# Softmax denominators from ScalarE's accumulator, and queries turned before they are split

## The reference

```python
qs, ks, vs = (relu(t.reshape(bs, ts, 16, 32)) for t in (layernorm(x), ctx, ctx))
att = softmax(einsum('bthf,byhf->bhty', qs, ks) / sqrt(32))
out = einsum('bhty,byhf->bhtf', att, vs).reshape(bs, ts, -1)
x = x + tanh(g_xattn) * relu(out @ ffn_w.T + ffn_b)
# then, on layernorm(x): xr, xk = token-shift mixes
x = x + tanh(g_ffn) * sigmoid(xr @ W_r.T) * (square(relu(xk @ W_k.T)) @ W_v.T)
```

## Time and profile before

| what | value |
|---|---|
| three timed runs, median (lowest to highest) | 2979.16 us (2978.43 to 2980.26) |
| the profiled execution: time, span | 2980.25 us, 2978.4 us |
| TensorE, VectorE, ScalarE, GpSimd busy | 96%, 78%, 53%, 35% |
| mean granted TensorE clock | 0.993 |
| HBM traffic over the span | 137 GB/s |

### The profile page before, as it was taken

The page is one execution under the profiler, slowest core; times in us unless marked ns, Lnnn a source line. Parts: engine busy times, 40 slices in busy tenths (PEclk is TensorE's granted clock), DMA queues, the critical chain, the costliest instruction groups (busy, mean ns, idle before and its releaser), DMA issues.

```text
span 2978.4 us, 71298 instructions
## 1 busy us (share of the span) xinstructions
PE 2860.3 (96%) x23168; PEld 2190.6 (74%) x23168; DVE 2330.1 (78%) x4175; ACT 1564.3 (53%) x2828; POOL 1045.4 (35%) x902
## 2 busy tenths in 40 slices
PE   3899999999999999999999999999999999999998
PEld 2677777777777777777777777777777777777776
DVE  5777877878878878878877877877878778788774
ACT  4445555555455455555555555555555555554552
POOL 0233333333343343333333333333333333333434
PEclk9899999999999999999999999999999999999999
DMA  5544445445445445445445445455455454454431
GB/s 168 150 122 140 144 124 155 140 127 155 135 131 156 137 131 154 133 137 150 131 142 149 128 143 153 120 149 152 120 152 146 124 152 142 124 156 137 130 109 41
DMA packets 405258, 408.56 MB, mean 137 GB/s; under 512 B 164577, under 2 KB 329441, under 8 KB 405218
## 3 DMA queue, kind: packets, MB, share of 16 engines
q1 hardware_dynamic: 352994, 340.92, 39.6%
q10 hardware_dynamic: 52224, 67.12, 7.3%
HBM read 272.64 MB, written 134.22 MB: 137 GB/s over the span
## 4 chain that ended last, share of the span: by engine, by line
PE 59%; DVE 16%; DMA 10%; SPq 7%; issue 5%; ACT 1%; ACTq 1%; DVEq 0%; POOL 0%; POOLq 0%
PE bank L951 29%; DMA out_dram<-x 8%; PE bank L918 7%; PE bank L932 6%; PE bank L906 5%; PE bank L944 4%; DVE m_nat L699 4%; DVE o_val L718 4%; SPq L272 3%; DVE st L652 3%; DVE k_raw L682 2%; PE bank L893 2%; PE bank L875 2%; SPq L258 2%; SPq L270 2%
## 5 line engine op out<-in xcount | busy, mean ns | idle before, releaser
L496 ACT ACTIVATE probs<-bank 128x512 f32<-128x512 f32 x1024 | 596.4, 594 | 455.7 <-PE bank L918 228.1
L699 DVE TENSOR_REDUCE m_nat<-bank 128x2 fp32r<-128x512 f32 x1024 | 695.4, 685 | 107.4 <-PE bank L906 106.7
L477 ACT ACTIVATE q_st<-bank 96x512 fp32r<-96x512 f32 x512 | 304.1, 594 | 718.9 <-PE bank L875 718.8
L918 PE MATMUL bank<-q_st,k_st 97*128 97x256 f32 x2048 | 449.9, 301 | 64.2 <-ACT probs L496 47.4
L718 DVE RECIPROCAL o_val<-bank 128x256 f32<-128x256 f32 x256 | 449.1, 1754 | 56.1 <-PE bank L944 51.7
L918 PEld LDWEIGHTS bank<-q_st,k_st 97*128 97x128 f32 x2048 | 341.8, 191 | 153.8 <-issue 58.5
L906 PE MATMUL bank<-k_st,q_st 96*128 96x256 f32 x2048 | 431.6, 293 | 7.4 <-DMA k_st<-k_dram 4.8
L397 POOL TENSOR_TENSOR xm<-xm 128x512 f32<-128x512 f32 x128 | 133.3, 1041 | 787.2 <-ACT xm L540 787.2
L906 PEld LDWEIGHTS bank<-k_st,q_st 96*128 96x128 f32 x2048 | 358.2, 192 | 59.8 <-issue 6.2
L708 DVE CAST m_t<-bank 4x256 fp32r<-4x256 f32 x256 | 105.1, 411 | 285.5 <-PE bank L884 285.4
L364 POOL TENSOR_TENSOR o_lo<-o_mv,o_hi 128x512 fp32r<-128x512 f32 x128 | 164.8, 1287 | 430.0 <-ACT o_hi L503 430.0
(11 more groups left out here) (90 smaller groups left out, 6026.6 us busy)
## 6 DMA issues: line engine op xcount, KB each, us to landing
k_st<-k_dram SPq DMA_DIRECT2D x256, 256.0 KB, 3.6
k_raw<-ctx_t_dram SPq DMA_DIRECT2D x256, 128.0 KB, 3.0
x_ln<-x_dram SPq DMA_DIRECT2D x256, 128.0 KB
k_dram<-k_high SPq DMA_DIRECT2D x64, 512.0 KB, 3.0
k_dram<-k_raw SPq DMA_DIRECT2D x64, 512.0 KB, 4.5
k_st<-k_dram SPq DMA_DIRECT2D x256, 128.0 KB, 3.5
o_dram<-o_val SPq DMA_DIRECT2D x256, 128.0 KB, 1.7
o_mv<-o_dram SPq DMA_DIRECT2D x512, 64.0 KB, 2.2
```

What stands on the lines that cost most here:

```text
L477: nc.scalar.activation(q_st[0:QK, c, :, P * u:P * u + P], tp_bank[0:QK, :].rearrange("p (g t) -> p g t", g=GR), ACT.Copy).then_inc(q_stack ...
L496: nc.scalar.activation(probs[:, n // GR % 2, n % GR, :, :].rearrange("p v t -> p (v t)"), st_bank[n % 2][:, :], ACT.Exp, scale=SCALE).then ...
L699: nc.vector.tensor_reduce(m_nat[:, c % 2, :, n % GR:n % GR + 1], s_bank[n % 2][:, :].rearrange("p (u y) -> p u y", u=NU), AX_X, ALU.max, n ...
L918: mm = nc.tensor.matmul(st_bank[n % 2][:, T * v:T * v + T], k_st[0:ST, c, g, P * v:P * v + P], q_st[0:ST, c, g, :], start=True, stop=True)
```

## The change

**Denominators.** `denominators` is gone, `values` alone fills `pv_bank`. Instead ScalarE's new `sum_exp(b, n)` takes the exponent of the natural scores in place in `s_bank`, with the negated maximum as bias, once for each half of the tokens, and its accumulator output goes to a column of `den`. So a bank of scores is free for the next head only after `s_summed`, no longer after `s_maxed`. `recip` inverts the eight columns of a group, `turn_rden` turns them, `copy_rden` copies them out of the bank, SyncE writes them to `rden_dram` and reads them back spread over the rows (`rd_val`), and `norm_o` multiplies by that.

**Queries.** `norm_1` writes a reordered tile `q_low_t`, with the softmax scale in it (the variance is multiplied by 32). `turn_q` turns it unsplit, twice a round, four full tiles in fp32; `q_high` and `q_low` split it from the bank, and `write_q` and `stack_q` take both parts through `q_dram`, as the keys go.

**Maxima.** One turn for both halves of a group instead of two.

```diff
+            def sum_exp(b, n):
+                if on(b):
+                    act.wait_ge(s_maxed, HEADS * b + n + 1)
+                    c, g = n // GR, n % GR
+                    for u in range(NU):
+                        scores = s_bank[n % 2][:, T * u:T * u + T]
+                        last = nc.scalar.activation(scores, scores, ACT.Exp, bias=m_nat[:, c % 2, g, u:u + 1].bitcast(F32),
+                                                    accum_out=den[:, c, NU * g + u:NU * g + u + 1])
+                    last.then_inc(s_summed, 1)
...
             def q_high(b, u):
                 if on(b):
+                    act.wait_ge(q_turned, NU * b + u + 1)
+                    nc.scalar.activation(x_ln[:, u, :].bitcast(F32R), tp_bank[:, :], ACT.Relu).then_inc(q_hi_ready, 1)
...
+            def recip(b, c):
+                if on(b):
+                    dve.wait_ge(s_summed, HEADS * b + GR * c + GR)
+                    nc.vector.reciprocal(rden[:, c, :], den[:, c, :]).then_inc(rden_ready, 1)
...
-                    nc.vector.reciprocal(o_val[:, :], pv_bank[:, T:2 * T]).then_inc(rden_ready, 1)
-                    dve.wait_ge(rden_ready, CH * b + c + 1)
-                    nc.vector.tensor_tensor(o_val[:, :], pv_bank[:, 0:T], o_val[:, :],
+                    dve.wait_ge(rd_moved[c], 16 * (b + 1))
+                    nc.vector.tensor_tensor(o_val[:, :], pv_bank[:, 0:T], rd_val[:, c, :],
...
                 if on(b):
+                    pe.wait_ge(x_normed, NU * b + u + 1)
                     freed(*users)
+                    for c in range(KC):
+                        mm = nc.tensor.transpose(tp_bank[:, P * c:P * c + P],
+                                                 q_low_t[:, u, c, :],
+                                                 ident_r[:, :].bitcast(F32))
                     mm.then_inc(q_turned, 1)
...
-                    after(pe, s_maxed, HEADS * b + n - 1)
+                    after(pe, s_summed, HEADS * b + n - 1)
...
-                turns = [("q", i, 2, 1), ("m", i, 1, 0), ("q", i, 3, 0), ("q", i, 3, 1),
+                turns = [("m", i, 1), ("q", i + 1, 0), ("q", i + 1, 1), ("rden", i, 1), ("m", i, 2),
+                         ("rden", i, 2), ("x", i - 1, 0), ("m", i, 3), ("x", i - 1, 1), ("rden", i, 3),
+                         ("m", i + 1, 0), ("rden", i + 1, 0)]
...
                     if kind == "q":
-                        return q_stacked, b, 2 * CH, 2 * c + u + 1
+                        return q_lo_ready, b, NU, n + 1
```

More of the change, by code:

```diff
@@ L139, in flamingo_block @@
         q_turned = sem("q_turned")
-        q_stacked = sem("q_stacked")
+        q_written = sem("q_written")
+        q_stacked = [sem(f"q_stacked{c}") for c in range(CH)]
         v_ready = sem("v_ready")
@@ L152, in flamingo_block @@
         pv_ready = sem("pv_ready")
+        s_summed = sem("s_summed")
         rden_ready = sem("rden_ready")
+        rden_turned = sem("rden_turned")
+        rden_copied = sem("rden_copied")
+        rden_written = sem("rden_written")
+        rd_moved = [sem(f"rd_moved{c}") for c in range(CH)]
         o_ready = sem("o_ready")
@@ L931, in values @@
                             h = GR * c + g
-                            nc.tensor.matmul(pv_bank[HD * g:HD * g + HD, 0:T], v_pos[:, v, HD * h:HD * h + HD],
-                                             probs[:, c % 2, g, v, :], start=(v == 0), stop=(v == NU - 1))
-            def denominators(b, c):
-                if on(b):
-                    after(pe, o_ready, CH * b + c)
-                    sums = [[probs[:, c % 2, g, v, :] for g in range(GR)] for v in range(NU)]
-                    for n, per_head in enumerate(sums):
-                        for g, moving in enumerate(per_head):
-                            mm = nc.tensor.matmul(pv_bank[HD * g:HD * g + HD, T:2 * T], ones_r[:, 0:HD].bitcast(F32),
-                                                  moving, start=(n == 0), stop=(n == len(sums) - 1))
+                            mm = nc.tensor.matmul(pv_bank[HD * g:HD * g + HD, 0:T], v_pos[:, v, HD * h:HD * h + HD],
+                                                  probs[:, c % 2, g, v, :], start=(v == 0), stop=(v == NU - 1))
                     mm.then_inc(pv_ready, 1)
@@ L1059, in iteration @@
                 values(i - 1, 3)
-                turn(1)
-                denominators(i - 1, 3)
+                turn(0)
                 dense(0, 2)
@@ L1064, in iteration @@
                 dense(0, 3)
-                turn(2)
+                turn(1)
                 shifted_scores(i, 2)
@@ L1070, in iteration @@
                 dense(1, 1)
+                turn(2)
                 shifted_scores(i, 3)
-                turn(3)
                 dense(1, 2)
@@ L1076, in iteration @@
                 dense(1, 3)
+                turn(3)
                 shifted_scores(i, 4)
@@ L1088, in iteration @@
                 turn(4)
-                denominators(i, 0)
                 shifted_scores(i, 6)
-                turn(5)
                 dense(3, 0)
@@ L1105, in iteration @@
                 scores(i, 15)
-                turn(7)
                 dense(4, 1)
@@ L1127, in iteration @@
                 dense(5, 3)
-                turn(11)
+                turn(9)
                 shifted_scores(i, 12)
@@ L1137, in iteration @@
                 values(i, 2)
-                turn(12)
+                turn(10)
                 scores(i + 1, 4)
@@ L1144, in iteration @@
                 scores(i + 1, 5)
-                denominators(i, 2)
-                turn(13)
                 dense(7, 1)
@@ L1152, in iteration @@
                 dense(7, 3)
+                turn(11)
             pipeline(pe, iteration)
```

197 lines of the change are left out of this document (125 added, 72 removed).

## The result

The changed kernel takes 3493.72 us (median of four timed runs, 3471.76 to 3495.93), the kernel before 2978.80 in the same comparison: ratio 1.171, 95% interval 1.166 to 1.176. The forecast was 2865, and the range ended at 3015. The change makes the kernel slower by 17%.

The account below looks back on a forecast made before the run. TensorE's own work was taken as the bound, 44.27 of 44.95 us a round. Work of 38.8 plus waits of 2.2, 1.65 and 0.5 gave 43.15 us, hence 2865 us; range 2803 to 2958, with outer end 3015.

Parts of the forecast that it names:

- TensorE's work, 38.8 us a round: TensorE's own work after denominators and old query turns leave and new turns enter: 38.8 us, from 44.27.
- The summing exponent, 0.50 us: ScalarE's 32 new 128x256 exponents with accumulator output, taken at 0.50 us each, 16 us a round.
- Rival 2: Slower kernel because ScalarE's summing exponent is long; decides from 0.76 us each, up to 3086 us; chance 0.15.
- The two waits on the turning bank, 2.2 and 1.65 us: TensorE waits for VectorE's low part at the second query turn, 2.2 us, and the reciprocals' turn, 1.65 us.
- The third wait, 0.5 us: Scores two heads on wait for a sum where tanh, copies and the keys' relu load ScalarE: 0.5 us a round.
- the sum 38.8 + 2.2 + 1.65 + 0.5: TensorE's work plus three waits: 43.15 us a round, 1.8 less than 44.95.
- rival 4: Busy DMA engines and SyncE's 55 in-order transfers land the query stack late; 2993 us at 8.5 us landing; chance 0.07.
- Rival 3, the clock: Idle gaps lower TensorE's clock; 1.8 us of work a round at 1.2 GHz eats the gain; chance 0.09.
- The wait at 1043.93 left the clock at 1.00: Argument against the clock loss: TensorE's existing 0.64 us wait for ScalarE's exponent had not lowered the clock.
- The forecast's own first wait, 2.2 us: TensorE at the second query turn, waiting for VectorE's low part to free the turning bank: 2.2 us a round.
- DMA share 0.7 to 0.75: DMA engines' busy share with 3.0 MB more a round: 32 of 43 us, 75%; sign of being right: near 0.7.
- That alone is no bound: Claim that DMA engines busy 32 of 43 us a round, 75%, do not by themselves limit the kernel.

Follow-up runs that it names:

- e10: Changed kernel without the reciprocals' DRAM trip and the division, maxima moved by ScalarE's queue, four query calls early: 3063.91 us, ratio 1.028.
- e8: Kernel before with ScalarE's sums replacing the denominators, old queries, no DRAM trip, division left out: 3137.71 us, ratio 1.053.
- e4: Kernel before with the queries' new way alone, denominators still by TensorE: 3236.19 us, ratio 1.086.
- e12: e8 with three of the four small copies of turned sums moved forward on VectorE: 3087.83 us, ratio 1.036.
- e1: Changed kernel without the reciprocals' trip through DRAM, multiplying by ones, so the division is left out: 3181.45 us, ratio 1.068.
- e2: Changed kernel with SyncE's order alone changed: reads behind the next move of maxima, loads behind the last: 3303.54 us, ratio 1.109.
- e3: Changed kernel with the four moves of maxima issued from ScalarE's queue instead of SyncE's: 3494.73 us, ratio 1.173.
- p1: Kernel before with TensorE paused once a round until one small ScalarE operation behind head 4's exponent is done: 3251.87 us, ratio 1.092.
- e13: e8 with sums ahead of each slot's exponent and three of the four small copies moved forward: 3083.07 us, ratio 1.034.

## Why the prediction was wrong, step by step

**TensorE's work, 38.8 us a round: about right.** The changed kernel shows 42.6 at a clock of 0.94. Taking 0.06 x 53.1 = 3.2 us off for the clock leaves 39.4. e10 leaves 40.0. Of the 5.5 us of work that the forecast took off (44.27 to 38.8; its 6.2 held 0.7 of idle time too), 4.3 to 4.9 are seen to go. e8 shows less, 2.5 of the 3.9 us expected of it (42.3 less 0.5 for the clock, against 44.3). Part of what is missing may be only how busy time is counted: in e4's timeline a matmul of 0.28 us is followed by the next after 0.12, but before a gap it counts whole. With over seven gaps a round in e8 instead of one, that is about 1 us, an estimate that no run checks.

**The summing exponent, 0.50 us: right.** Two groups of the page, the exponent and its read-out, and two neighbours in ScalarE's timeline:

```profile
L551 ACT ACTIVATE bank<-bank,m_nat 128x256 f32<-128x256 f32 x2048 | 921.4, 453 | 169.1 <-DVE m_nat L767 168.8
...
L551 ACT ACTIVATION_READ_ACCUMULATOR bank<-bank,m_nat 128x1 f32 x2048 | 434.2, 212 | 0.0
```

```profile
1507.22 0.45 ACT L551 ACTIVATE bank<-bank,m_nat 128x256 f32<-128x256 f32 x1
1507.58 0.20 ACT L551 ACTIVATION_READ_ACCUMULATOR bank<-bank,m_nat 128x1 f32 x1
1507.67 0.45 ACT L551 ACTIVATE bank<-bank,m_nat 128x256 f32<-128x256 f32 x1
```

From start to start it is 0.45 us with the read-out, which largely lies beside the exponent. Rival 2 (0.76 us and more) did not happen. ScalarE comes to 2180.8 / 64 = 34.1 us a round, 35.4 in the forecast.

**The two waits on the turning bank, 2.2 and 1.65 us: right in place and cause, 2.1 and 1.0 in size.** The tenth of a microsecond at the first is partly luck. In the round shown TensorE is ready for the turn 8.1 us after the round's first shifted score instead of 7.6, and starts it 10.4 us after instead of 9.8, because the two normalisations take 1.3 us instead of 0.9 and TensorE had stood 0.26 at the first query turn. At the second the chain from turn to turn took 3.9 us for the 4.0 worked out, but the work that TensorE has in between ran partly at the lower clock and filled more of it (a wait of 0.19 us there, 1.0 on average).

**The third wait, 0.5 us: small in the changed kernel** (8.6 us over the span), because other waits give ScalarE time. In e12 it is 3.1 us, but e12 keeps the old queries' copies, with 37.9 us of ScalarE's work a round against 34.0 here. e10, with the new queries, runs as fast as e12 and shows 8.7 us over the span. So what it would be in the whole change at the forecast's pace is open.

**The step that failed: the sum 38.8 + 2.2 + 1.65 + 0.5 had no term for the wait on the row of maxima.** It had only the two waits on the bank and one on the sums. SyncE's 55 transfers instead of 35 were counted in rival 4, and there only for the stack of queries, with a chance of 0.07. The move of the maxima stands in the same queue, is needed within the round, and cost 6.6 us a round. Two things were left out of its walk: that SyncE stops at each read-back until its write has landed (746.0 us over 254 reads, 2.9 each), and that the row, once issued, takes 2.3 to 5.9 us to land among the loads. The landing of the keys and the issue of the maxima were both at hand; the chain from copy to shifted scores was never made from them. Relieving the queue (e1) gave 312 us and reordering it (e2) 190, while taking only the maxima out of it (e3) gave nothing: it is what the whole queue has to do in a round, and in which order. Rival 4's own object, the stack of queries, held TensorE for only 18.2 us over the span. The Trainium skill, DMA: Bandwidth & Descriptors, section "Anatomy of one DMA — SWDGE (gpsimd) path", says for another path that the fixed cost of a transfer is mostly the confirmation that its last byte has landed, slowest in HBM. These writes carry 8 rows of 512 bytes and are still waited for 2.9 us on average; the trace does not separate the confirmation from the time behind other transfers, and the write issued at 1528.80, behind four loads, held SyncE until 1535.09.

**Rival 3, the clock: dismissed on a row that could not decide it.** "The wait at 1043.93 left the clock at 1.00" was true of 0.64 us. The forecast's own first wait, 2.2 us, is nearly as long as p1's pause, and that cost 1.8 us beyond its length. The wait of 2.31 us in the changed kernel is followed by slices at 0.63 and 0.80, 3 x 0.37 + 3 x 0.20 = 1.7 us. So with no surprise in SyncE's queue the sum comes to 43.15 + 1.7, about 44.9 us, an estimate: no gain worth the name. The rival's arithmetic was right (1.8 us of work at the lower level eats the gain), its chance of 0.09 was the error. In the changed kernel the clock took about 3.2 us a round. That is an estimate from its mean; the same working gives 2.5 for p1 (0.05 x 49.5), where the busy time grew by 2.0.

**The sum again**, from what was measured: 38.8 + 0.6 + 3.2 (clock) + 10.6 (waits) = 53.2 us against 53.1; 8.1 us more than before over 64 rounds are about 520 us, for 515 measured. The 0.6 is what the busy time and the clock's estimate leave over, so the sum closes by its making; what it shows is the sizes. The two terms that the forecast did not have, 6.6 us for the maxima and 3.2 for the clock, are 9.8 of the 10.0 us between 43.15 and 53.1; the smaller differences cancel.

**DMA share 0.7 to 0.75: 0.62,** because the same bytes are spread over a longer round: 0.62 x 53.1 = 32.9 us of all engines, where 32 had been worked out. **"That alone is no bound": right**, since e10 runs faster at 0.67.

**What stays open.** Whether any order of the whole scheme reaches the kernel before was not shown. The runs above tried few orders. e10 and e13 leave out the division and still end 3% above it, each with 4.6 to 5.6 us of idle TensorE a round in several pieces. That dropping the denominators takes work off TensorE is shown by the busy times (2.0 to 2.5 us a round in e8); that it can be had as time is not.

## What to carry to other kernels

Before pricing work that leaves the bounding engine, walk every chain that feeds it back to where it starts, in-order DMA queues included, and for each queue list what now stands ahead of the one small transfer that the bound waits for. In a round with no slack, a read that must wait for its own write belongs on a queue where nothing urgent stands behind it. And price a wait on TensorE at more than its length: here a gap of 2.5 us cost 4.3.

## What the runs showed of the hardware

- Gaps of 2.31, 3.11, 4.18 and 2.55 us were followed by slices of 3 us with a granted clock of 0.63, 0.50, 0.56 and 0.60, that is partly at 1.2 GHz, although TensorE was then busy without a pause. The price beyond the gap grew from 1.8 to 2.4 us as it grew from 2.45 to 3.49. The Trainium skill, TensorE: Matmul & The Clock Gate, section "Why this matters for your kernels", warns of idle gaps between bursts; this trace agrees. Many short gaps cost little clock: e12, with 4.5 us idle a round in pieces of 1.37 us and less in the round looked at, kept 0.99.
- ScalarE's accumulator is read by an instruction of its own, 0.21 us, of which 0.09 show from start to start.
- A row of 4 KB on SyncE's queue took 2.3 us from issue to release of its reader in one case and 5.9 behind four loads and four stack transfers in another; from ScalarE's queue in e10 it was 4.9 once (1522.30 to 1527.24).
